# Experts' second layer with channels on the partitions, softmax scaling after the heads

## The reference

```
# 1. row-wise convolutional LSTM over 16 rows, 48 features, then a 1x1 skip conv
x = x + conv1x1(lstm_rows(conv_masked(x)), w_skip) + b_skip
# 2. attention over the 256 pixels of a sample as tokens: 6 heads of 16, causal
t = tokens(x);  n = layernorm(t)
p = softmax(mask(q(n) k(n)^T * 96**-0.5))
t = t + concat_heads(p v(n)) @ Wp + bp
# 3. mixture of 4 experts, the best 2 per token
n = layernorm(t)
probs = softmax(n @ gate_w + gate_b);  g = top2(probs) / (sum(top2(probs)) + 1e-9)
h_e = gelu(n @ w1_e + b1_e)            # 96 -> 384, exact gelu
t = t + sum_e g_e * (h_e @ w2_e + b2_e)  # 384 -> 96
```

## Time and profile before

| | us |
|---|---|
| median of 3 runs | 464.43 (464.39 to 466.17) |
| the profiled execution's own time | 466.77 |
| its span in the trace | 465.0 |
| busy: TensorE matmul | 435.8 |
| busy: TensorE weight load | 347.0 |
| busy: VectorE | 269.5 |
| busy: ScalarE | 263.6 |
| busy: GpSimd | 145.8 |

### The profile page before, as it was taken

The page is one execution under the profiler, slowest core; times in us unless marked ns, Lnnn a source line. Parts: engine busy times, 40 slices in busy tenths (PEclk is TensorE's granted clock), DMA queues, the critical chain, the costliest instruction groups (busy, mean ns, idle before and its releaser), DMA issues.

```text
span 465.0 us, 10797 instructions
## 1 busy us (share of the span) xinstructions
PE 435.8 (94%) x3199; PEld 347.0 (75%) x3199; DVE 269.5 (58%) x954; ACT 263.6 (57%) x740; POOL 145.8 (31%) x309
## 2 busy tenths in 40 slices
PE   6999998759899999999999999999999999999897
PEld 6999996436568777877777778678767877787676
DVE  3888888535525852775277437634763585266424
ACT  2544454336477648664865585567657764865370
POOL 5000000425422542362255315531542254235200
PEclk9999999997999999999999999999999999999999
DMA  8600000021021002101210120022002100200000
GB/s 200 134 0 0 0 0 1 25 68 27 1 61 28 19 15 67 39 0 37 52 30 0 45 51 22 0 51 51 17 0 59 42 0 13 68 22 1 15 4 18
DMA packets 14393, 14.95 MB, mean 32 GB/s; under 512 B 5426, under 2 KB 11412, under 8 KB 14372
## 3 DMA queue, kind: packets, MB, share of 16 engines
q1 hardware_dynamic: 14180, 14.30, 12.3%
q0 software_dynamic: 192, 0.39, 0.3%
HBM read 3.86 MB, written 1.57 MB: 12 GB/s over the span
## 4 chain that ended last, share of the span: by engine, by line
PE 74%; DVE 12%; ACT 5%; issue 5%; SPq 2%; DMA 1%; POOL 1%; DVEq 1%; ACTq 0%; POOLq 0%
PE F L1026 19%; PE T L984 9%; PE A L1005 8%; PE F L1042 4%; PE S L968 4%; PE F L1046 4%; PE F L1043 3%; PE S L970 3%; PE F L1022 3%; PE S L973 2%; DVE c L629 2%; DVE ig L627 2%; ACT tc_sb L471 2%; DVE pt_sb L457 1%; PE M L947 1%
## 5 line engine op out<-in xcount | busy, mean ns | idle before, releaser
L406 POOL TENSOR_SCALAR p_sb<-p_sb,rden 128x128 f32<-128x128 f32 (+1 forms) x192 | 79.3, 427 | 133.4 <-DVE rden L710 131.2
L1026 PE MATMUL F<-w_sb,hid 128*128 128x96 f32 x768 | 101.0, 276 | 0.0
L1026 PEld LDWEIGHTS F<-w_sb,hid 128*128 128x128 f32 x768 | 93.4, 192 | 5.9 <-issue 5.9
L518 ACT ACTIVATE p_sb<-S,nmax 128x128 f32<-128x128 f32 (+1 forms) x192 | 78.8, 425 | 17.4 <-DVE nmax L704 17.3
L704 DVE TENSOR_REDUCE nmax<-S 128x2 f32<-128x512 f32 (+1 forms) x80 | 50.7, 634 | 53.1 <-PE S L973 52.8
L457 ACT COPY pt_sb<-T 128x512 f32<-128x512 f32 (+1 forms) x48 | 26.4, 550 | 69.2 <-PE T L984 69.2
L564 ACT ACTIVATE hid<-F,b_sb 128x512 f32<-128x512 f32 x72 | 49.3, 686 | 8.2 <-PE F L1046 7.5
L1005 PE MATMUL A<-pt_sb,v_cur 128*32 128x128 f32 x576 | 44.2, 284 | 8.4 <-ACT pt_sb L457 4.5
L984 PE MATMUL T<-id_sb,p_sb 128*128 128x128 f32 x288 | 49.3, 290 | 1.4 <-POOL p_sb L406 1.4
L968 PE MATMUL S<-k_bd,q_st 96*128 96x384 f32 (+2 forms) x96 | 38.7, 410 | 4.8 <-DMA k_bd<-k_cur 3.8
L984 PEld LDWEIGHTS T<-id_sb,p_sb 128*128 128x128 f32 x288 | 30.9, 143 | 16.2 <-issue 14.1
(11 more groups left out here) (142 smaller groups left out, 793.8 us busy)
## 6 DMA issues: line engine op xcount, KB each, us to landing
k_bd<-k_cur SPq DMA_DIRECT2D x96, 32.0 KB, 2.0
q_st<-q_cur SPq DMA_DIRECT2D x28, 96.0 KB, 2.2
k_bd<-k_cur SPq DMA_DIRECT2D x96, 16.0 KB, 1.8
t_st<-t_cm SPq DMA_DIRECT2D x7, 192.0 KB, 2.4
out_y<-y_sb SPq DMA_DIRECT2D x7, 192.0 KB, 1.9
x_pad<-in_x SPq DMA_DIRECT2D x2, 612.0 KB, 9.0
w_sb<-in_w SPq DMA_DIRECT2D x1, 576.0 KB
hid<-in_w SPq DMA_DIRECT2D x1, 576.0 KB, 7.5
```

The source lines that it names most:

```text
L406: last = nc.gpsimd.tensor_scalar(p, p, rden[:, u % 3, i:i + 1], 1.0, ALU.mult, ALU.mult)
L518: last = nc.scalar.activation(p_sb[:, u % 3, i * nk:(i + 1) * nk], S[u % 2][:, i * nk:(i + 1) * nk], ACT.Exp, bias=nmax[:, u % 3, i:i + 1] ...
L1026: last = mm(dst[:, e * C:(e + 1) * C], hid[:, c, s * TT:(s + 1) * TT], w2_sb[:, c], start=False, stop=(c == NCH - 1), skip_group_check=True)
```

## The change

- The second layer is turned: `w2_sb[:, c]` (128 x 96) is the weights and `hid[:, c]` with all 512 tokens the moving operand, so it is 12 products of 512 columns instead of 48 of 96 with four bias products. The output has channels on the partitions, one expert a bank: `Y` = F0, F1, F0, F1. Expert 2 waits for expert 0's bank, expert 3 for expert 1's.
- `FILL` becomes 4, 0, 1, 0, 1, 0, 1, 0, 1, 0; of the four left, one goes ahead of project_q, two after project_out(3), one after the transposition of `xh2`.
- `combine` works by expert: (bank + bias column) times the gates, then an addition in SBUF. Experts 0 and 1 are combined by VectorE in slots 5 and 7, expert 2 after attn_residual(3) ahead of q's rest, expert 3 after `x2lo`. TensorE transposes the sum back into bank T, `turn_y`, between chunks 5 and the route's transposition, and `finish` adds `t1p` after `route(n, 0)`.
- The gates must lie along the tokens on every channel's partition: TensorE transposes `gw` in slot 1 (`turn_gates`), ScalarE copies it, SyncE writes 16 x 128 values to HBM and reads them back repeated on 96 partitions (`spread_gates`), ahead of `stage`.
- GpSimd no longer scales the probabilities. The row sums of a tile's six heads are collected, VectorE takes one reciprocal a tile, GpSimd spreads it to 16 columns a head (`spread`), TensorE turns it into bank F2 (`turn_sums`), ScalarE copies it (`take_spread`), and VectorE multiplies it onto the heads (`heads_out`, from ScalarE to VectorE).
- F2 (`R`, `GT`) serves the sums and the gates, so the first layer's banks are `L1` = F2, A, F0, F1. The bias in hi and lo parts, its setup on three engines and the two-part last store go.

```diff
-FILL = [16, 3, 3, 2, 3, 3, 2, 2, 2, 0]
-TAIL = SPB * NCH - sum(FILL)
-TAIL_EARLY = min(TAIL, 9)
+FILL = [4, 0, 1, 0, 1, 0, 1, 0, 1, 0]
+TAIL = NCH - sum(FILL)
+TAIL_FIRST, TAIL_EARLY = 1, 3
+COMBINE_AT = (5, 7)
...
-        L1 = [F[0], A, F[1], F[2]]
-        L2 = [F[0], F[2], F[1], F[2]]
+        L1 = [F[2], A, F[0], F[1]]
+        Y = [F[0], F[1], F[0], F[1]]
+        GT = R = F[2]
...
+            def spread_gates(n, first=False):
+                wait_alone(sp, gate_copied, n + 1)
+                sp.dma_start(gate_hbm.rearrange("e s t -> s e t"), gate_t[:]).then_inc(gate_out, 16)
+                wait_alone(sp, gate_out, 16 * n + 16)
+                if not first:
+                    wait_alone(sp, gated, E * n)
+                sp.dma_start(gates_cm[:], gate_hbm.rearrange("e s t -> (e s t)").unsqueeze(0).to_broadcast((C, E * BT))
+                             ).then_inc(gate_in, 16)
...
-            def scale(n, u):
-                wait_alone(pool, rden_done, NU * n + u + 1)
...
-                for i in range(HG[t]):
-                    p = p_sb[:, u % 3, i * nk:(i + 1) * nk]
-                    last = nc.gpsimd.tensor_scalar(p, p, rden[:, u % 3, i:i + 1], 1.0, ALU.mult, ALU.mult)
-                last.then_inc(scaled, 1)
+            def spread(n, s, first=False):
+                wait_alone(pool, rden_done, 4 * n + s + 1)
+                if s or not first:
+                    wait_alone(pool, spread_ready, 4 * n + s)
+                nc.gpsimd.tensor_copy(rden_c[:], rden[:, s % 2].unsqueeze(2).to_broadcast((128, HEADS, HS))
+                                      ).then_inc(rden_spread, 1)
...
-            def heads_out(n, s, first=False):
-                act.wait_ge(av_ready, NU * n + TILE_END[s])
+            def take_spread(n, s, first=False):
+                act.wait_ge(spread_ready, 4 * n + s + 1)
...
+                nc.scalar.copy(rden_t[:], R[0:C, 0:TT]).then_inc(spread_done, 1)
+            def take_gates(n):
+                act.wait_ge(gate_turned, n + 1)
+                nc.scalar.copy(gate_t[:], GT[0:SPB * E, 0:TT]).then_inc(gate_copied, 1)
...
+            def heads_out(n, s, first=False):
+                dve.wait_ge(av_ready, NU * n + TILE_END[s])
...
+                dve.wait_ge(spread_done, 4 * n + s + 1)
+                V.tensor_tensor(o_t[:], A[0:C, 0:TT], rden_t[:], ALU.mult).then_inc(ot_done, 1)
...
+            def combine(n, e, first):
+                dve.wait_ge(y_ready, E * n + e + 1)
+                if e == 0:
+                    dve.wait_ge(gate_in, 16 * n + 16)
...
+                dst = y_part[:, e % 2] if e else y_cm[:]
+                V.scalar_tensor_tensor(dst, Y[e][0:C, :], b2_sb[:, e:e + 1], gates_cm[:, e], ALU.add, ALU.mult
+                                       ).then_inc(gated, 1)
+                if e:
...
+                    V.tensor_tensor(y_cm[:], y_cm[:], dst, ALU.add).then_inc(summed, 1)
+            def finish(n, first):
+                dve.wait_ge(y_turned, n + 1)
+                dve.wait_ge(t1p_done, n + 1)
...
+                V.tensor_tensor(y_sb[:], T[:, 0:SPB * C].rearrange("p (s c) -> p s c", c=C), t1p[:], ALU.add
+                                ).then_inc(y_done, 1)
...
+            def turn_sums(n, s, first=False):
+                pe.wait_ge(rden_spread, 4 * n + s + 1)
...
+                if s == 0 and not first:
+                    pe.wait_ge(gate_copied, n)
+                mm(R[0:C, 0:TT], rden_c[:].rearrange("p r d -> p (r d)"), id_sb[:], start=True, stop=True
+                   ).then_inc(spread_ready, 1)
...
+                for c in parts:
+                    e = c // CPE
+                    dst = Y[e]
+                    if c % CPE == 0:
+                        if e >= 2:
+                            pe.wait_ge(gated, E * n + e - 1)
...
+                    last = mm(dst[0:C, :], w2_sb[:, c], hid[:, c, :], start=(c % CPE == 0), stop=(c % CPE == CPE - 1))
...
+            def turn_y(n):
+                pe.wait_ge(summed, (E - 1) * n + E - 1)
+                for s in range(SPB):
+                    last = nc.tensor.transpose(T[:, s * C:(s + 1) * C], y_cm[:, s * TT:(s + 1) * TT], id_sb[0:C, 0:C])
...
+            expert_out(NBLK - 1, range(2 * CPE))
+            turn_gates(NBLK - 1)
+            expert_out(NBLK - 1, range(2 * CPE, NCH))
+            turn_y(NBLK - 1)
```

More of the change, by code:

```diff
@@ L267, in out_parts @@
         def out_parts(slot):
-            return [divmod(i, NCH) for i in range(sum(FILL[:slot]), sum(FILL[:slot + 1]))]
+            return range(sum(FILL[:slot]), sum(FILL[:slot + 1]))
         def wait_alone(eng, semaphore, value):
@@ L350, in body @@
                 load_keys(1, 1)
+                if not first:
+                    spread_gates(n - 1, first=not store)
                 if more:
@@ L547, in body @@
                         take_x1(n + 1)
-                heads_out(n, SPB - 1, first)
+                    if j == 1 and not first:
+                        take_gates(n - 1)
+                take_spread(n, SPB - 1, first)
                 if not last:
@@ L784, in body @@
                     route(n - 1, 1)
-                recip(n, 0)
                 if first:
@@ L792, in body @@
                         row_max(n, j + 2)
-                    if j + 1 < NU:
-                        recip(n, j + 1)
+                    for s in range(SPB):
+                        if j + 2 == TILE_END[s]:
+                            recip(n, s)
+                        if j == TILE_END[s]:
+                            heads_out(n, s, first)
                     if j not in PT_ON_ACT:
@@ L798, in body @@
                         x1_rest(n + 1)
-                    if not first and j:
-                        for s, c in out_parts(j - 1):
-                            if c == NCH - 1:
-                                combine(n - 1, s, second)
+                    if not first and j in COMBINE_AT:
+                        combine(n - 1, COMBINE_AT.index(j), second)
                     if not last:
@@ L812, in body @@
                             normalize2(n, s)
+                heads_out(n, SPB - 1, first)
                 attn_residual(n, SPB - 1)
+                if not first:
+                    combine(n - 1, 2, second)
                 if not last:
@@ L821, in body @@
                 if not first:
-                    for s in range(sum(FILL[:-1]) // NCH, SPB):
-                        combine(n - 1, s, second)
+                    for e in range(3, E):
+                        combine(n - 1, e, second)
                 route(n, 0)
+                if not first:
+                    finish(n - 1, second)
                 if not last:
@@ L842, in _ @@
             route(NBLK - 1, 2)
-            for s in range(SPB):
-                combine(NBLK - 1, s, False)
+            for e in range(E):
+                combine(NBLK - 1, e, False)
+            finish(NBLK - 1, False)
         @block.tensor
@@ L1037, in expert_hidden @@
                         pe.wait_ge(ot_done, 4 * n + 4)
-                    elif not first:
-                        pe.wait_ge(comb, 16 * n - 16 + 4 * (c + 1))
+                    elif L1[c] is not R and not first:
+                        pe.wait_ge(gated, E * n - E + 1 + max(e for e in range(E) if Y[e] is L1[c]))
                     cs = slice(c * 128, (c + 1) * 128)
@@ L1055, in body @@
                             expert_out(n - 1, out_parts(j))
+                        for s in range(SPB - 1):
+                            if j == TILE_END[s]:
+                                turn_sums(n, s, first)
                         values(n, j - 1, first)
@@ L1083, in body @@
                             project_out(n, s)
+                if not first:
+                    expert_out(n - 1, tail[0:TAIL_FIRST])
                 if not last:
```

143 lines of the change are left out of this document (76 added, 67 removed).

## The result

The changed kernel takes 492.37 us (median of 4 runs, 491.79 to 493.75) beside 464.44 for the kernel before on the same chip (4 runs, 464.39 to 466.17). The ratio of the times is 1.060, with a 95% interval from 1.056 to 1.063: it is 28 us slower. Forecast were +22 us and a range of 466 to 496. The profiled execution took 491.79 us with a span of 490.0. An execution more than 1.5% above the fastest of its kernel is left out of the ratios (one of e4, three of d4), but not out of the medians.

A forecast was written before the change was run, and what follows sets the result against it. TensorE, busy 43.1 of 44.1 us in a middle block, was taken as the bound. Blocks +16.1, first block -1.5 and ending +7.3 gave +21.9 on the profiled 466.77, so 486 us on the median; range 466 to 496.

The forecast's parts named there:

- The sum: Whole kernel: blocks +16.1, first block -1.5, after the last block +7.3, together +21.9 us on the profiled execution.
- TensorE's work hardly moves: TensorE's work per block: cheaper products against added transpositions, a fall of only 0.5 us, at 0.43 us a 512-column pass.
- A middle block: Each of blocks 1 to 7: slots +0.3, end part +1.65, first layer +0.35, together +2.3 us.
- The slots' term: Ten attention slots of a middle block: 2.05 us less fill against added waits, taken as +0.3 us.
- wait of product 6: Slot 6: expert 2's first product waits for bank F0 until VectorE combines expert 0, 1.8 us (1.0 to 2.2).
- the gates' wait: Slot 2: the sum turning waits until ScalarE has copied the gates, 0.5 us (0 to 0.9).
- The block's end: Last transposition to first layer: +1.0, then +0.65 from TensorE's 1.4 us wait before xh2's transposition; together +1.65 us.
- Gates through HBM: Gates' write about 2 us, read 4.5 to 7; adds 0, at worst 3 us a block.
- First block: No experts there; 1.4 us of TensorE waits for GpSimd and their echo go: -1.5 us, between -3 and 0.
- After the last block: Last six products wait for the gates' DMA and expert 0's combine: +7.3 us (+5 to +10), clock fall left out.
- Rival 1: TensorE stays the bound and the waits are hidden: -0.5 us a block, 466.7 us in all; chance 0.13.
- Rival 3: Second layer's 512-column pass costs 0.23 us, not 0.43; about -2.5 us a block, 451 us in all; chance 0.08.

The follow-up runs named there:

- e4: Changed kernel with the softmax scaling back on GpSimd and no turning of sums, turned second layer kept: 487.43 us, ratio 1.044 to the kernel before.
- d4: d3 with its two waits, before xh2 and x2hi, filled by products nobody reads: 455.76 us (6 runs); ratio 0.972, from three of them.
- e2: Changed kernel with VectorE's combine of expert 2 moved behind x2's rest: 486.89 us, ratio 1.044 to the kernel before.
- d3: Kernel before with hid and w2 rounded to fp32r in the second layer, one pass a product: 463.76 us, ratio 0.996 to the kernel before.
- c2: Changed kernel with e1, e2 and e3 together, plus second-layer products spread again (slot 1, behind project_out(3)): 466.21 us, ratio 1.001 to the kernel before.
- e5: Changed kernel with hid and a copy of w2 rounded to fp32r, one pass a product: 493.78 us, ratio 1.058 to the kernel before.
- c3: c2 with the softmax scaling back on GpSimd: 465.11 us, ratio 0.997 to the kernel before.
- e1: Changed kernel with product 6, the first of expert 2, moved from slot 6 to slot 7: 483.49 us, ratio 1.037 to the kernel before.
- e3: Changed kernel with free banks S0 and S1 for experts 2 and 3 after the last block: 487.61 us, ratio 1.046 to the kernel before.
- d1: c3 with the last block's second layer by tokens as in the kernel before, no gates through HBM there: 461.70 us, ratio 0.993 to the kernel before.

## Why the prediction was right, and where sizes were off

- **The sum.** Forecast +21.9 between the profiled executions, measured +25.0: the blocks +17.3 for 16.1, the first part -2.4 for -1.5, the ending +10.1 for 7.3. On the medians 486 was forecast and 492.4 came. Half of that miss is these terms, the other half that the profiled execution of before is slower than its median and that of after is not.
- **TensorE's work hardly moves.** Right. A plain fp32 pass of 512 columns takes 0.43 us, as worked out from the rows of 96 and 128 columns, and busy time fell by 3 us in eight blocks.
- **A middle block.** Forecast +2.3, measured +2.85. The mean of the seven distances, +2.47, is nearer only because the last costs 0.6. By parts, from TensorE's timeline in a middle block of each trace:

| part of the block | before | after | change | forecast |
|---|---|---|---|---|
| fill to the last transposition | 25.50 | 26.18 | +0.7 | +0.3 |
| from there to the first layer | 6.76 | 8.63 | +1.9 | +1.65 |
| first layer to fill | 11.94 | 12.24 | +0.3 | +0.35 |

- **The slots' term was too small.** The wait of product 6 was put at 1.8 and measures 1.30, the gates' wait at 0.5 and measures 0.28. Both are smaller, yet the slots cost 0.4 more than taken. The term that was too small is the work. The prediction counted about 0.05 us at each group's start for the kernel before and none after, and put a lone product at 0.86 and a sum turning at 0.25. In the timeline a lone product takes 0.95 to 1.03 and a sum turning 0.31 to 0.39; four and three of them are about 0.7 us. The smaller waits hide part of it.
- **The block's end.** The mechanism was right: a wait of 1.4 was forecast and is 1.54. The combine's two instructions take 0.74 and 0.69 us where 0.66 and 0.6 were put. e2 confirms the place: with the combine gone from it, the wait falls by 0.9.
- **Gates through HBM.** Right: the read takes 5.0 us (4.5 to 7 forecast), is hidden in middle blocks and makes a pause of 7.9 us after the last.
- **First block.** Forecast -1.5, measured -2.4, but most of it is luck. In the profiled execution of before the clock is at its lower level from 103 to 109, and in that of after it is at 1.00 there. d3 has no second layer in its first block either, and so the same work as before; its clock stays at 1.00 there, and its first mark comes at 127.6 instead of 129.4; in d4, again with the same first block, the clock falls at about 103 and the mark comes at 129.2. So 1.8 of the 2.4 us go with the clock of one execution, and the scaling is worth about 0.6. That clock may also be why this execution of before took 2.3 us more than the median; no second trace of before shows it.
- **After the last block.** Forecast +7.3, measured +10.1. The step that failed is leaving the clock's fall out of the sum although showed one after far shorter waits. Its price was off too: 5.1 was put, 2.3 came, because the clock rose again within the burst. The rest of the chain was right: from the first product to expert 0's combine 13.4 us (13.25 forecast), from the last product to the end 5.1 (5.0).
- **Rival 1** did not happen, but c2 shows that it could have: the same work in another order costs nothing.
- **Rival 3.** Its condition, a pass of 0.23 us, did not hold. Its price of 451 isn't borne out either: it charged 2.5 of 4.8 us a block to waits and nothing to the clock. In e5, which saves 7.5, waits took 4.7 and the clock 3.4, and the run came to 493.78. A saving of just 4.8 was not run.
- **Only counting TensorE's queue was half the truth.** The prediction read the bound from 43.1 busy of 44.1 us. In d3 5.5 us less work on TensorE moved nothing: 2.1 us turned into waits for VectorE, ScalarE and GpSimd, and 3.5 went to the lower clock that came behind them. d4 separates the two: with the clock at 1.00 a block is 2.7 us shorter, so no chain of the other engines holds a block at 44 us. What the 48 small products were worth was their cover, and the turned layer keeps the work and gives the cover up.

**Which half costs what.** In the order of the change, giving the scaling back to GpSimd is worth 1.5% (e4); in a better order about 0.4% (c2 against c3, whose intervals overlap by a thousandth), which is hardly to be told from nothing. The rest is the place of expert 2's first product, of its combine, and the ending (e1 to e3), and the places of the other products (c2). d1, with the turned layer in seven blocks, GpSimd's scaling and the old ending, gains 0.7%.

## What to carry to other kernels

When many small products become a few large ones, list first what each small group was covering, then place the large ones and count every bank that they must wait for: here that, and not the work, was the whole loss. A busy share near 100% does not say that less work is less time; halve the work once and read how much of it comes back as waits and as a lower granted clock. Where the clock falls behind a short wait that can't be removed, filling the wait with products that nobody reads can be worth trying, over many executions: here it brought 2 to 3% in three of six. And before a difference between two profiles is put down to the change, compare their clocks: 1.8 us of this one's first block were the clock's.

## What was unexpected of the hardware

- The granted clock fell to its lower level behind two waits of 0.83 and 0.48 us at a block's end in d3, but not behind one of 1.54 us in the changed kernel, where the products around it are plain fp32 passes of 512 columns. Near 144 and 232 in d3 and near 228 in d4 it fell with TensorE recorded as busy (1.91 and 2.00 of 2.00 us in d4). The runs show that filling the waits helped in three executions of six, not what the rule is.
- Behind such a fall the lower level stayed for 6 to 7 us in e5 and in the rows of d3 above, while TensorE worked without pause, at 0.43 instead of 0.23 us a product of 512 columns. It isn't always that long: behind the fall near 232 in d3 it stayed for about 10 us of unbroken work, behind that near 228 in d4 for about 3.
- On VectorE the 96x512 combine from PSUM took 0.74 us and the addition of the same size from SBUF alone 0.69. They are different instructions, but with all operands in SBUF only 0.05 us was saved.
